# Spectral products of all batches in the setup, setup tables on ScalarE and GpSimd, and clears ordered around the powers

## What is computed

```python
mtr = _orthogonalize_mode_to_rank(mode_to_rank)      # 64 x 64, by a Cholesky factor
proj = einsum('bsd,kd->bsk', x, input_basis) * spectral_coeff[:, None, :]
hidden = einsum('bsk,kr->bsr', proj, mtr) * rank_coeff[:, None, :]
x = x + einsum('bsr,ro->bso', hidden, output_basis)
```

## Time and profile before

| what | us |
|---|---|
| median of 3 runs | 1674.92 (1671.84 to 1675.13) |
| profiled execution, its own time | 1671.96 |
| its span | 1670.1 |
| TensorE busy | 1558.0 (93%) |
| VectorE busy | 1029.1 (62%) |
| ScalarE busy | 766.6 (46%) |
| GpSimd busy | 176.2 (11%) |

### The profile page before, as it was taken

How to read it: one execution, slowest core, us unless ns; L and a number is a source line. 1 busy time by engine, 2 the same in 40 slices (tenths; PEclk the granted TensorE clock), 3 DMA queues, 4 the chain that set the end, 5 groups by cost and what they waited for, 6 DMA issues and landing times. The chain is left out here.

```text
span 1670.1 us, 30670 instructions
## 1 busy us (share of the span) xinstructions
PE 1558.0 (93%) x11020; PEld 1287.9 (77%) x11020; DVE 1029.1 (62%) x3377; ACT 766.6 (46%) x1657; POOL 176.2 (11%) x206
## 2 busy tenths in 40 slices
PE   2189999999999999999999999999999999999996
PEld 1067888888888888888888888888878788787884
DVE  6765555555555555555556776776766766667663
ACT  0035444344444444433345555555555555555554
POOL 9000000000000000000000000000000110111102
PEclk9999999999999999999999999999999999999999
DMA  4074232333223332132223544544544534445340
GB/s 165 13 93 81 42 50 45 52 52 52 37 37 52 52 50 44 30 58 40 39 39 78 72 62 62 72 63 63 71 62 60 87 63 74 77 69 82 68 69 21
DMA packets 99776, 100.09 MB, mean 60 GB/s; under 512 B 11670, under 2 KB 96280, under 8 KB 98986
## 3 DMA queue, kind: packets, MB, share of 16 engines
q1 hardware_dynamic: 99626, 98.14, 36.5%
HBM read 16.83 MB, written 4.19 MB: 13 GB/s over the span
## 5 line engine op out<-in xcount | busy, mean ns | idle before, releaser
L881 ACT ACTIVATE work<-bank 128x512 f32<-128x512 f32 x768 | 455.6, 600 | 263.4 <-PE bank L1071 249.4
L576 DVE TENSOR_REDUCE rowmax<-bank 128x2 f32<-128x512 f32 x512 | 343.6, 687 | 135.8 <-PE bank L1054 129.8
L1071 PE MATMUL bank<-qs,ks 98*128 98x256 f32 x1536 | 401.9, 344 | 0.0
L1054 PE MATMUL bank<-ks,qs 96*128 96x256 f32 x1536 | 359.1, 316 | 8.9 <-DVE rowmax L573 5.6
L1071 PEld LDWEIGHTS bank<-qs,ks 98*128 98x128 f32 x1536 | 271.4, 192 | 30.9 <-issue 13.2
L1054 PEld LDWEIGHTS bank<-ks,qs 96*128 96x128 f32 x1536 | 246.0, 190 | 53.6 <-issue 18.9
L1083 PE MATMUL bank<-work,vp 128*32 128x256 f32 x3072 | 193.1, 383 | 0.0
L573 DVE CUSTOM_DVE_ANT_0 xt_in<-bank,big_q 128x256 bf16<-128x256 f32 x512 | 191.4, 421 | 0.3 <-issue 0.3
L907 ACT ACTIVATE work<-bank 128x256 f32<-128x256 f32 x128 | 49.1, 384 | 244.6 <-PE bank L1130 244.6
L1130 PE MATMUL bank<-yt,w_gate 128*128 128x256 f32 x512 | 134.5, 384 | 5.0 <-DVE qk_lo L542 3.7
L1083 PEld LDWEIGHTS bank<-work,vp 128*32 128x32 f32 x3072 | 86.2, 109 | 64.6 <-ACT work L881 6.7
(11 more groups left out here) (205 smaller groups left out, 1859.9 us busy)
## 6 DMA issues: line engine op xcount, KB each, us to landing
qs<-qk_hi SPq DMA_DIRECT2D x192, 128.0 KB, 3.9
ks<-qk_hi SPq DMA_DIRECT2D x192, 128.0 KB, 4.4
qs<-qk_lo SPq DMA_DIRECT2D x96, 128.0 KB, 4.4
ks<-qk_lo SPq DMA_DIRECT2D x96, 128.0 KB, 4.3
x_in<-in_x SPq DMA_DIRECT2D x16, 256.0 KB, 4.9
xt_in<-in_x_t SPq DMA_DIRECT2D x16, 256.0 KB, 5.0
out<-xres SPq DMA_DIRECT2D x16, 256.0 KB, 2.1
qs<-nm SPq DMA_DIRECT2D x96, 16.0 KB
```

Of the source, the lines that this page charges most:

```text
L576: a = dve.tensor_reduce(rowmax[:, :, k:k + 1], bank[:, :].rearrange("p (t s) -> p t s", t=TC), AX, ALU.max)
L881: act.activation(probs[:, place[n, b, k], :, :], bank[:, :].rearrange("p (c s) -> p c s", c=TC), ACT.Exp, scale=HD ** -0.5)\
L1054: m = pe.matmul(bank[:, t * S:(t + 1) * S], qs[par][0:SCORE_ROWS, k, t * P:(t + 1) * P], ks[par][0:SCORE_ROWS, k, :], start=True, stop=True)
L1071: m = pe.matmul(bank[:, c * S:(c + 1) * S], ks[par][0:SHIFTED_ROWS, k, c * P:(c + 1) * P], qs[par][0:SHIFTED_ROWS, k, :], start=(n != 3), ...
```

## The change

1. Spec leaves the pipeline. In the setup TensorE computes the spectral products of all 16 batches, in banks 0 and 1 in turn, and ScalarE scales each into the first half of that batch's own `xres`, from which rank reads it. `xres` is empty until cond writes it, so it also holds x transposed: four transfers of 1 MB each, ahead of the weights of layer 1, in place of 16 loads into xt_in. Products 8 to 11 wait for the 21st step of elimination C, 12 to 15 for the 28th.
2. What "tables", "mod rows", "norm" and "turned" did on VectorE is done in the setup by ScalarE (identity, masks, keys, mean, squares, copies) and GpSimd (silu, pick, the variance and its power, gains, the residues of the modulation rows). VectorE keeps "ortho", "top" and "shares"; "spread" goes to ScalarE. TensorE's product for the modulation rows and its two for the field stand ahead of and between the spectral products.
3. GpSimd's clears are now 24, in another order: ten small ones, then five large ones, and the others between its new instructions; the power of A comes after 19 of them and the last five stand between the two powers.
4. `w_basis` and `rms_rows` lie in the tile of `yt`, and the exponentials of batch 0 no longer wait for the field.
5. Slots: layer 1's xT goes from -25.61 to -26.52, rank from -33 to -32.36, the second neg from 1.59 to 2.53 and others less; in layer 2 the second pair of PV groups from 17.26 to 16.53, wo from 24.47 to 25.09; in layer 3 smax, k and the last stack a little later, resid earlier.

```diff
-        "smax": -13.9, "pv": (5.73, 9.68, 12.87, 16.61), "neg": (-6.41, 1.59), "max": (-6.11, 3.88), "xT": -25.61, "q": -24.35,
-        "stack": (-25.3, -22.08, -15.9, -16.88), "k": -22.83, "v": -12.2, "tok": 18.52, "load": -46, "spec": -34, "rank": -33,
+        "smax": -13.9, "pv": (5.73, 9.68, 12.87, 16.05), "neg": (-6.41, 2.53), "max": (-6.11, 4.83), "xT": -26.52, "q": -24.35,
+        "stack": (-25.3, -22.08, -15.9, -16.03), "k": -22.83, "v": -12.2, "tok": 18.52, "load": -46, "rank": -32.36,
...
-ONCE = {"ortho": -33.5, "tables": -32.2, "mod rows": -25.5, "norm": -22.0, "turned": -20.0, "top": -18.0, "shares": -16.0, "spread": -14.5}
+ONCE = {"ortho": -33.5, "top": -30.3, "shares": -26.5, "spread": -22.0}
...
+            for g in range(NBATCH // 4):
+                sp.dma_start(xres[:, 4 * g:4 * (g + 1), :, :], ins["x_t"][4 * g:4 * (g + 1)].rearrange("b p c s -> p b c s")).then_inc(s_xt[g], 16)
...
-                        sp.dma_start(xt_in[:], ins["x_t"][b]).then_inc(x_loaded.sem, 16)
...
+            clear(0, 15)
...
+            clear(15, 18)
...
+            clear(18, 19)
...
+            root("A")
...
+            pool.tensor_tensor(fld[:, 1, :], fld[:, 1, :], ln_gb[:, 0, :], ALU.mult).then_inc(s_fld_n, 1)
...
+            pool.tensor_tensor(mod_rest[:], mod_rest[:], mod_parts[:], ALU.subtract).then_inc(s_mod_rest, 1)
+            pool.wait_ge(s_mod_rest, 1)
+            clear(19, CLEARS)
...
             root("C")
...
+            act.copy(ident_bf[:], ident[:]).then_inc(s_tables, 1)
+            act.activation(big_q[:], mask_q[:], ACT.Copy, scale=BIG).then_inc(s_tables, 1)
+            act.activation(big_k[:], mask_k[:], ACT.Copy, scale=BIG).then_inc(s_tables, 1)
...
+            for b in range(NBATCH):
+
+                act.wait_ge(s_spec, b + 1)
+                act.activation(xres[:, b, 0, :], banks[b % 2][:, 0:S], ACT.Identity, scale=cvec[:, SPEC, b:b + 1]).then_inc(h_spec_ok.sem, 1)
...
+            pe.matmul(banks[5][:, :], silu3[:], w_mod[:], start=True, stop=True).then_inc(s_mod, 1)
+            pe.wait_ge(s_memset, SMALL_CLEARS)
+            for b in range(NBATCH):
+
+                if b % 4 == 0:
+                    pe.wait_ge(s_xt[b // 4], 16)
+                if b in (8, 12):
+
+                    pe.wait_ge(s_vch, mark["C", (20, 27)[b // 12]])
+                if b >= 2:
+                    pe.wait_ge(h_spec_ok.sem, b - 1)
+                for c in range(DC):
+                    m = pe.matmul(banks[b % 2][:, 0:S], w_basis[:, c, :], xres[:, b, c, :], start=(c == 0), stop=(c == DC - 1))
+                m.then_inc(s_spec, 1)
...
-                    if what == "spec":
...
-                            m = pe.matmul(bank[:, 0:S], w_basis[:, c, :], xt_in[:, c, :], start=(c == 0), stop=(c == DC - 1))
...
+                        pe.matmul(bank[:, 0:S], mtr[:], xres[:, b, 0, :], start=True, stop=True).then_inc(head.sem, 1)
```

More of the change, by code:

```diff
@@ L185, in __call__ @@
                 return piece.rearrange(f"p ({' '.join(names)}) -> p {' '.join(names)}", **dict(zip(names, shape[1:])))
-        setup, ffn = Carver(work), Carver(work)
+        yt = sb("yt", [P, DC, S])
+        setup, ffn, setup_late = Carver(work), Carver(work), Carver(yt[:, :, :].rearrange("p c s -> p (c s)"))
         ffn.at = n_probs
@@ L276, in cond_resid_kernel @@
         fld_t = setup([P, DC, NBATCH])
-        th_c = setup([C, NBATCH])
+        th_c, less = setup([C, NBATCH]), setup([C, NBATCH])
+        eps = setup([NBATCH, 1])
         s_first, s_ld0, s_ld = sem("s_first"), sem("s_ld0"), {n: sem(f"s_ld{n}") for n in LAYERS}
@@ L284, in cond_resid_kernel @@
         s_mtr, s_rank, s_tables, s_raw_field, s_var, s_rstd, s_fld, s_fld_t = (sem(f"s_{a}") for a in ("mtr", "rank", "tables", "raw_field", "var", "rstd", "fld", "fld_t"))
-        s_silu, s_mod = sem("s_silu"), sem("s_mod")
+        s_silu, s_silu3, s_mod, s_mod_row, s_mod_scaled, s_mod_part, s_mod_rest = (sem(f"s_{a}") for a in ("silu", "silu3", "mod", "mod_row", "mod_scaled", "mod_part", "mod_rest"))
+        s_xt = [sem(f"s_xt{g}") for g in range(NBATCH // 4)]
+        s_pick, s_spec, s_keys, s_some, s_mean, s_fld_n = (sem(f"s_{a}") for a in ("pick", "spec", "keys", "some", "mean", "fld_n"))
         s_fs, s_top, s_exp, s_shares, s_fa, s_field = (sem(f"s_{a}") for a in ("fs", "top", "exp", "shares", "fa", "field"))
@@ L344, in banks_of @@
                     return [(head, what, self.qk_lo, "qk".index(what) + 1)]
-                reader = {"spec": (h_spec_ok, 1), "rank": (h_rank_ok, 1), "cond": (x1_ok, 1), "xT": (self.xt, DC),
+                reader = {"rank": (h_rank_ok, 1), "cond": (x1_ok, 1), "xT": (self.xt, DC),
                           "v": (self.vp, 1), "coh1": (c1_ok, DC), "coh2": (zz_ok, 1), "oT": (self.ot, DC), "yT": (yt_ok, DC)}
@@ L736, in _ @@
         def _(pool):
-            clears = [(half[:], -0.5), (ones[:], 1.0), (guard[:], 1e-6), (cvec[:], 0.0), (cvec[C:CA, SILU, :], 1.0)]
+            clears = [(half[:], -0.5), (ones[:], 1.0), (guard[:], 1e-6), (cvec[:], 0.0), (cvec[C:CA, SILU, :], 1.0),
+                      (w_basis[:, :, C:P], 0.0), (w_outb[C:P, :], 0.0), (mtr[:], 0.0), (silu3[:], 0.0), (eps[:], 1e-5)]
+            assert len(clears) == SMALL_CLEARS
             for i in range(2):
@@ L741, in _, with clear @@
                            (ks[i][96:98, :, :].bitcast(F32), 1.0), (vp[i][:, :, :, HD:HW], 0.0), (vp[i][:, :, :, HD:HD + 1], 1.0)]
-            clears += [(w_basis[:, :, C:P], 0.0), (w_outb[C:P, :], 0.0), (mtr[:], 0.0), (silu3[:], 0.0)]
+            assert len(clears) == CLEARS
+            def clear(first, end):
+                for k in range(first, end):
+                    if k:
+                        pool.wait_ge(s_memset, k)
+                    pool.memset(*clears[k]).then_inc(s_memset, 1)
             def root(name):
@@ new lines, in _ @@
+            pool.tensor_tensor(cvec[0:C, SILU, :], th_c[:], less[:], ALU.mult).then_inc(s_silu, 1)
+            pool.wait_ge(s_silu, 1)
+            clear(15, 18)
+            pool.wait_ge(s_memset, 18)
+            pool.wait_ge(s_first, 16 * len(loads_first))
+            for g in range(P // HC):
+                column = HC * g % (P - HC)
+                pool.tensor_copy(pick[HC * g:HC * (g + 1), :], ident[HC * g:HC * (g + 1), column:column + NBATCH]).then_inc(s_pick, 1)
+                pool.wait_ge(s_pick, g + 1)
@@ new lines, in _ @@
+            clear(18, 19)
+            pool.wait_ge(s_memset, 19)
+            pool.wait_ge(s_var, 1)
+            pool.tensor_tensor(fs[:, 2:3], fs[:, 1:2], eps[:], ALU.add).then_inc(s_var, 1)
+            pool.wait_ge(s_var, 2)
+            pool.tensor_tensor(fs[:, 3:4], fs[:, 2:3], half[0:NBATCH, 0:1], ALU.pow).then_inc(s_rstd, 1)
+            pool.wait_ge(s_rstd, 1)
+            root("A")
+            pool.wait_ge(s_root, 1)
+            pool.wait_ge(s_fld_n, 1)
+            pool.tensor_tensor(fld[:, 1, :], fld[:, 1, :], ln_gb[:, 0, :], ALU.mult).then_inc(s_fld_n, 1)
@@ L761, in step @@
                 def step(what, k, b, par):
-                    if what == "norm":
-                        pool.wait_ge(s_var, 1)
-                        pool.tensor_tensor(fs[:, 3:4], fs[:, 2:3], half[0:NBATCH, 0:1], ALU.pow).then_inc(s_rstd, 1)
                     if what == "squares" and n == 1:
@@ L1143, in step @@
                         if b == 0:
-                            pe.wait_ge(s_vch, mark["mod rows"])
+                            pe.wait_ge(s_mod_part, 4)
+                            pe.wait_ge(s_pick, P // HC)
                             pe.wait_ge(attn2_ok.sem, attn2_ok.at(NBATCH, 0))
```

195 lines of the change are left out of this document (93 added, 102 removed), and 10 rows, old and new, of the table SLOT.

## The result

The changed kernel takes 1645.08 us (median of 4, 1644.56 to 1647.76) against 1674.99 for the kernel before on the same chip: ratio 0.9829 [0.9812, 0.9846], faster by 1.7%. The forecast was 1645. The profiled execution has a span of 1643.4 us against 1670.1: 26.7 us less, where the sum said 28.2.

A forecast was written before the change was run, and what follows sets the result against it. TensorE's own stream bounds the layers; in the setup it waits on a chain of small VectorE steps. Terms summed to 28.2 us off 1671.96, giving 1643.8; with medians 3 us above the profiled execution, the forecast was 1645, range 1633 to 1658.

The forecast's parts named there:

- GpSimd beside VectorE: Setup: GpSimd instructions reading SBUF during the eliminations cost 0; 3.6 us lost if VectorE stood for half their time.
- First power: Setup: with large clears moved behind it, VectorE's wait falls from 4.68 to 0.74 us, saving 3.9 us.
- Products late: Setup: the 16 spectral products lie under the second elimination and end 0 to 2.5 us late, taken as 0.4.
- Tables, exponential, rank and cond: Setup: tables off VectorE save 2.5 us, faster rank and cond 1.5; the field's exponential ahead of ScalarE's squares costs 1.3.
- Ramp: Before batch 0's scores: q and k run as before, but scores begin at the low clock, losing 1.5 us (0 to 3).
- Layer 1: Spec's matmuls leave 14 batches at 0.86 us each, 12.0 us; the earlier xT slot ends q's xt wait, 9.0 us.
- Rival 1: Layer 1: the xt wait comes back as another wait; gain 19 us, time 1654; chance 0.15.
- Layers 2 and 3: Moved slots gain 2.5 us over 32 batches, ends -5 and +6, the 6 being layer 3's waits gone.
- rival 3: Layers 2 and 3: a moved step makes TensorE wait more each batch; 41 us lost, time 1687; chance 0.05.
- rival 2: Setup gives nothing: GpSimd blocks VectorE, products late, slow clock; 5.7 to 7 us less, time 1651; chance 0.15.

The follow-up runs named there:

- Three_sums: Changed kernel with three more GpSimd 32x512 sums that read SBUF beside the second elimination; 1648.65 us, ratio 0.9858.
- three_clears: Changed kernel with three more GpSimd 32x512 clears, which read nothing, beside the second elimination; 1646.64 us, ratio 0.9839.
- late_residues: Changed kernel with GpSimd's four modulation-row instructions and ScalarE's copies for them moved from the second elimination into batch 0 of layer 1; 1643.92 us, ratio 0.9827.
- copy_first: Changed kernel with GpSimd's first large clear held until VectorE's first copy, of the identity, is done; 1642.49 us, ratio 0.9823.
- no_hold: Changed kernel without the two waits that spread the last eight spectral products over the second elimination; 1647.68 us, ratio 0.9844.
- warm_before_scores: Changed kernel with 12 matmuls of no use put ahead of the first score product; 1643.55 us, ratio 0.9821.
- rank_thrice: Changed kernel with the rank matmul made three times over in batches 2 to 15, restoring a spec's passes; 1658.27 us, ratio 0.9908.
- xt_back: Changed kernel with only layer 1's xT slot returned from -26.52 to -25.61; 1657.12 us, ratio 0.9906.
- layer3_slots_back: Changed kernel with the four changed slots of layer 3 put back as before; 1651.5 us, ratio 0.987.

## Why the prediction came out, step by step

**Rule and row.** The step that failed is "GpSimd beside VectorE: I take 0". The trace before had only clears beside the updates, and from "0.24 us with one beside it" I went on to instructions of another kind. Three_sums and three_clears tell the kinds apart, and late_residues gives back 2.7 us of the 3.1 that the elimination had grown. The bound of 3.6 for the sums held (3.1); I chose the wrong end. The Trainium skill, "SBUF — State Buffer", section on the two separate sides, had said this, and the runs agree: a stall as long as what is left of GpSimd's instruction. The section also names the other kind, VectorE instructions in a two-port mode, which exclude GpSimd instructions whether these read or not; that agrees with the copy (2.97 us beside a clear) and the yn scaling (1.63 us for two). Which mode the two ran in, the traces don't show. The trace before held both (the first copy at 1.63 us; of two equal scalings of yn the first at 1.37 us and the second at 0.34), and I looked at the update alone.

**First power.** The 3.9 us were there: GpSimd reaches the power at 36.28 and is the one that waits. 1.3 of them went to the first copy, on which the moved large clear now lies for longer. That price wasn't in the sum; copy_first gives it back, and 1.0 us more.

**Products late: -0.4.** They weren't; they end 0.8 us before the elimination's result (71.45 and 72.27). The longer elimination didn't give them the room, since their holds move with its steps: in late_residues, with 2.7 us less of it, they end at 68.76, again 0.8 us before the result is used (69.57). The forecast's own figures for the high clock, 67.0 against 67.8, had this 0.8; The 0.4 had been added for the low clock, and the last four products took 3.69 us, the high clock.

**Tables, exponential, rank and cond.** Right: the residual add stands directly behind cond (2.5 forecast, 2.5 measured); ScalarE's squares start 1.0 us behind the end of the add (forecast 1.3); rank and cond fell by 0.52 and 0.69 us, 1.2 of the 1.5. By no_hold the held products did it; but the 0.69 us of cond are this profile's, and four of the eleven with the holds have none of it. From the second elimination's end to the transposes of xn these made some -2.8 us, and with its 0.6 us of delay -2.2, where the steps up to there said -6.2.

**Ramp: -1.5.** The cold clock cost about that by warm_before_scores, but the step left out the other side. This is read from the two traces and not isolated by a run. "q and k run as before", I wrote, and took the field products and specs that left the ramp for free cover; in the trace they had gated q and the first scores. From transposes to batch 0's projection the ramp became 1.8 us shorter, not 1.5 longer. This error of +3.3 us hides most of the setup's -4.0.

**Layer 1.** Per batch the spec was 0.87 by rank_thrice (forecast 0.86) and the slot 9.1 us by xt_back (9.0). The count of the spec's batches was wrong: "batches 2 to 15 stand in the full stream". The steady period covers 12; periods 13 to 15 shrank by 0.95, 0.23 and -0.04. 12 x 1.38 + 1.14 = 17.7, the measured 17.8. And 1.38 is not 0.86 + 0.64 = 1.50 because the gate's wait grew by 0.25; the other 0.13 goes the other way (the q product, started without a wait, takes 1.89 us instead of 1.99, which is 0.1 of it). By the single edits the two make 0.87 + 0.67 = 1.54 us a period; the 0.16 between this and 1.38 belong to something that was not taken back alone, as the other moved slots of layer 1. Rival 1 happened to a third of its size: the gate's wait grew by 3.1 us where the xt wait was worth 9.0.

**Layers 2 and 3.** +2.5 with ends -5 and 6: measured 0 and 4.8 (layer3_slots_back 5.7). The 6 us that I named as an end, the waits of layer 3 in the earlier trace rows, was nearest the truth: the slots moved were theirs. Of rival 3 nothing showed. In layer 2 the moved slots brought nothing (376.5 and 376.4 us).

Of the signs that were named for being right, the wait before the first power's use (0.80 us), the add right behind cond, no wait of q for xt in the steady batches and a period shorter by 1.5 us (1.38) came. A step unchanged beside GpSimd did not, and an update longer than 0.24 us had been named as a sign of being wrong. The products end at 71.45 us instead of near 67, with the elimination.

In sum: -4.0 up to the transposes, +3.3 in the ramp, -3.2 in layer 1, +2.3 in layers 2 and 3, which makes 26.6 for 28.2. The total was met more closely than the terms deserve: rival 2 was right on GpSimd holding up VectorE in the setup, and it is luck that the ramp and layer 3 paid for it.

## What to carry to other kernels

When work goes to GpSimd because it is idle, look at what VectorE does at that time: here an instruction that reads SBUF was paid by the next VectorE instruction with two SBUF inputs (up to 0.90 us each), and a copy between SBUF tiles stood still even beside a clear (2.97 us for 0.17). Order the copy ahead of the clear and keep the reads out of a chain of dependent VectorE steps. Count what a change removes in periods of the stream, not in batches, and look at the first and last of them. Where a row of waits is named and the moved slot is its own, take it as the term rather than as the bound. And where one profile shows a product at the high clock behind an idle stretch, look at the same product in other profiles before counting on it.
